# Second attention of a two-layer image tower: the strips of Q and K travel in halves, the heads' scores are dealt out over the body, and the loop over images is written out

## What is computed

```python
q, k, v = jnp.split(src @ in_proj_w.T + in_proj_b, 3, axis=-1)      # 16 heads of 16
scores = jnp.einsum('bhqd,bhkd->bhqk', q, k) / math.sqrt(dh)
ctx = jnp.einsum('bhqk,bhkd->bhqd', jax.nn.softmax(scores, axis=-1), v)
dense_output = ctx.transpose(0, 2, 1, 3).reshape(b, s, d) @ out_proj_w.T + out_proj_b
QK = jnp.einsum('bqr,bkr->bqk', Q, K) / math.sqrt(R)
topv, topi = jax.lax.top_k(jax.nn.softmax(QK, axis=-1), 51)         # a fifth of 257
sparse_attn = zeros_with(topv).normalised()
sparse_output = jnp.einsum('bqk,bkd->bqd', sparse_attn, V)
fused = sig * dense_output + (1.0 - sig) * sparse_output
x = _layernorm(src + fused, ln1_g, ln1_b)
```

## Time and profile before

| | before |
|---|---|
| device time, median of 3 runs | 1273.41 us (1272.54 to 1274.91) |
| the profiled execution | 1266.08 us |
| its span, first to last instruction | 1264.3 us |
| busy over the span | PE 80%, DVE 61%, PEld 59%, POOL 37%, ACT 30% |
| granted TensorE clock, mean | 0.907 of full |
| maximum of a head, L2259 | 128 times 689 ns; idle before it 79.7 us, 79.1 of them until PE's L2503 |
| score matmuls of the heads, L2503 | 256 times 381 ns; idle before them 33.5 us, 19.3 of them until the DMA into fa_ks |
| exponential, L2051 | 128 times 588 ns; idle before it 79.1 us, 77.3 of them until PE's L2568 |

### The profile page before, as it was taken

The page is one execution under the profiler, slowest core; times in us unless marked ns, Lnnn a source line. Parts: engine busy times, 40 slices in busy tenths (PEclk is TensorE's granted clock), DMA queues, the critical chain, the costliest instruction groups (busy, mean ns, idle before and its releaser), DMA issues. The chain is left out here.

```text
span 1264.3 us, 21795 instructions
## 1 busy us (share of the span) xinstructions
PE 1014.5 (80%) x6656; PEld 745.1 (59%) x6656; DVE 765.5 (61%) x1825; ACT 382.2 (30%) x943; POOL 467.4 (37%) x576
## 2 busy tenths in 40 slices
PE   0157989789999965379889789888779997788887
PEld 0155777486776743246556556555369996465555
DVE  7975666554222237367577667556507775688884
ACT  0242433112222221143344344343224442222221
POOL 4972010154000016123233224121136774476664
PEclk9978999759999996689889999898889998899999
DMA  9904500133111112553363463462040000000000
GB/s 316 340 2 142 192 0 1 34 111 116 59 59 60 62 39 64 83 110 105 61 129 94 71 127 91 58 129 92 24 160 1 0 0 1 1 9 17 8 17 18
DMA packets 66590, 94.85 MB, mean 75 GB/s; under 512 B 9176, under 2 KB 58792, under 8 KB 65232
## 3 DMA queue, kind: packets, MB, share of 16 engines
q1 hardware_dynamic: 63312, 85.48, 25.8%
q0 software_dynamic: 3200, 8.43, 2.2%
HBM read 53.28 MB, written 40.34 MB: 74 GB/s over the span
## 5 line engine op out<-in xcount | busy, mean ns | idle before, releaser
L2259 DVE TENSOR_REDUCE fa_nm<-fa_ps 128x2 f32<-128x514 f32 x128 | 82.9, 689 | 79.7 <-PE fa_ps L2503 79.1
L1505 PE MATMUL ex_ps<-we_raw,ex_xT 128*128 x320 | 117.7, 491 | 0.0
L2051 ACT ACTIVATE fa_eT<-fa_ps 128x512 f32<-128x512 f32 x128 | 72.5, 588 | 79.1 <-PE fa_ps L2568 77.3
L2503 PE MATMUL fa_ps<-fa_ks,fa_qs 126*128 126x258 f32 x256 | 65.8, 381 | 33.5 <-DMA fa_ks<-fa_qk_rows 19.3
L3308 PE MATMUL qf_ps<-qf_wg,qf_xT 128*128 128x352 f32 x272 | 90.1, 481 | 2.0 <-ACT qf_xT L3149 1.4
L451 PE MATMUL tk_ps<-tk_u,tk_qb 64*32 64x64 f32 x1024 | 23.9, 268 | 70.5 <-POOLq L318 56.7
L2568 PE MATMUL fa_ps<-fa_qs,fa_ks 128*128 128x256 f32 x256 | 66.0, 351 | 17.5 <-ACT fa_eT L2051 17.5
L1419 DVE COPY ex_hT<-ex_ps 128x384 f32<-128x384 f32 x40 | 22.3, 558 | 92.5 <-PE ex_ps L1514 92.4
L2503 PEld LDWEIGHTS fa_ps<-fa_ks,fa_qs 126*128 126x128 f32 x256 | 46.7, 240 | 49.5 <-issue 29.8
L3308 PEld LDWEIGHTS qf_ps<-qf_wg,qf_xT 128*128 128x128 f32 x272 | 50.7, 195 | 37.4 <-issue 6.8
L2939 PE MATMUL ff_ps<-ff_xT,wg_f 128*128 128x128 f32 x544 | 66.2, 282 | 3.2 <-ACT ff_xT L2838 3.2
(11 more groups left out here) (493 smaller groups left out, 2380.4 us busy)
## 6 DMA issues: line engine op xcount, KB each, us to landing
x_rows<-tk_zero SPq DMA_DIRECT2D x8, 2176.0 KB, 17.5
we_raw<-in_L_ffn_W SPq DMA_DIRECT2D x24, 384.0 KB, 8.1
fa_qs<-fa_qk_rows SPq DMA_DIRECT2D x16, 514.0 KB, 8.2
fa_ks<-fa_qk_rows SPq DMA_DIRECT2D x32, 257.0 KB, 10.4
ex_xin<-x_rows SPq DMA_DIRECT2D x40, 128.0 KB, 2.0
y_rows<-ex_y SPq DMA_DIRECT2D x40, 128.0 KB, 1.7
fa_rsb<-fa_rs_rows SPq DMA_DIRECT2D x32, 132.0 KB, 2.8
fa_qk_rows<-fa_qhl SPq DMA_DIRECT2D x32, 128.5 KB
```

Source lines behind the costliest of these rows:

```text
L1505: last = mm(ps[:, bank + t % 2, 0:HD], xT[:, t % 2, k, :], raw[:, ds(e, 1), m, k * HD:(k + 1) * HD], start=(k == 0), stop=(k == KC - 1))
L2051: cp(eT[:, j % 8, :], ps[:, ST + j % 2, :], ACT.Exp).then_inc(z["e_ready"], 1)
L2259: nc.vector.tensor_reduce(nm[:, :, j], ps[:, b:b + 2, 0:TOK], AX.X, ALU.max, negate=True).then_inc(z["max_done"], 1)
L2503: last = mm(ps[:, b + t, 0:WID], qs[0:TOPS, p, head(j, 1 + t * P, P)], ks[0:TOPS, p, head(j, 0, WID)], start=True, stop=True)
```

## The change

- **Halves.** Everything between projection and strips is done by halves of eight heads: PE, ACT, DVE and POOL in the order Q0, K0, Q1, K1, and in SP's queue eight writes in that order, then the maxima's rows of group 1, then the reads Q0, K0, Q1, K1: two and four DMAs each, of half the columns. Each half has semaphores of its own. Head 0 waits for the first half, head 7 for the second.
- **Heads.** The heads of image u+1 stood in slots 10 to 17, two in each. They now stand in slots 5 to 16, one or two in each; DVE takes the maxima in the slot after. The class query goes from slot 8 to slot 5, ahead of the projection, its maximum on DVE to slot 5, its exponentials on ACT from behind turned score 9 to behind 6. POOL multiplies the class blocks ahead of `shared_context`. The round of slot 5 moves to slot 6. Sparse scores: slot 14; both value products: slots 16 and 17, with DVE's part of both in slot 17.
- **Bodies.** All eight are written out on every engine.

```diff
-    ROUNDS_AT = {0: 1, 1: 1, 3: 1, 4: 1, 5: 1, 7: 1, 8: 1}
+    ROUNDS_AT = {0: 1, 1: 1, 3: 1, 4: 1, 6: 1, 7: 1, 8: 1}
...
-    HEADS_AT = {10: (0, 1), 11: (2, 3), 12: (4, 5), 13: (6, 7), 14: (8, 9), 15: (10, 11), 16: (12, 13), 17: (14, 15)}
-    MAXES_AT = {11: (0, 1), 12: (2, 3), 13: (4, 5), 14: (6, 7), 15: (8, 9), 16: (10, 11), 17: (12, 13, 14, 15)}
+    HEADS_AT = {5: (0, 1), 6: (2,), 7: (3,), 8: (4, 5), 9: (6,), 10: (7,), 11: (8, 9), 12: (10,), 13: (11,), 14: (12,),
+                15: (13, 14), 16: (15,)}
...
     def staged(eng, body):
-        body(0, 0, True, True, True, True)
-        with eng.Fori(0, 2) as i:
-            body(2 * i + 1, 1, False, True, True, True)
-            body(2 * i + 2, 0, False, True, True, True)
-        for u in range(5, BATCH):
-            body(u, u % 2, False, u + 1 < BATCH, u + 2 < BATCH, False)
+        for u in range(BATCH):
+            body(u, u % 2, u == 0, u + 1 < BATCH, u + 2 < BATCH, u + 3 < BATCH)
...
-            def strips_out(u, p, part, a, ready, out, read):
-                sp.wait_ge(z[ready], u + 1)
+            def strips_out(u, p, part, a, c, ready, out, read):
+                sp.wait_ge(z[ready], 2 * u + c + 1)
                 if a == 0 and u >= 2:
                     sp.wait_ge(z[read], 32 * (part + 1) * (u - 1))
                 src, dst = (qhl, khl)[part], d["fa_qk"][part, p, a]
-                for c in range(KC):
-                    sp.dma_start(dst[:, 8 * c:8 * c + 8, :].rearrange("d h n -> h d n"), src[:, a, c, :]).then_inc(z[out], 16)
-
-            def strips_in(u, p, part, out, read):
-                sp.wait_ge(z[out], 64 * (u + 1))
+                sp.dma_start(dst[:, 8 * c:8 * c + 8, :].rearrange("d h n -> h d n"), src[:, a, c, :]).then_inc(z[out], 16)
+
+            def strips_in(u, p, part, c, out, read):
+                sp.wait_ge(z[out], 32 * (u + 1))
                 if u >= 2:
                     sp.wait_ge(z["st_ps"], N * (u - 1))
                 if u:
                     sp.wait_ge(z[read], 32 * (part + 1) * u)
+                cols = slice(8 * c * TOK, 8 * (c + 1) * TOK)
                 src = d["fa_qk"][part, p].rearrange("a d h n -> a d (h n)")
                 if part == 0:
                     for i in range(2):
-                        sp.dma_start(qs[2 * DH * i:2 * DH * (i + 1), p, :].bitcast(F32), src.rearrange("a d n -> (a d) n")
-                                     ).then_inc(z[read], 16)
+                        sp.dma_start(qs[2 * DH * i:2 * DH * (i + 1), p, cols].bitcast(F32),
+                                     src.rearrange("a d n -> (a d) n")[:, cols]).then_inc(z[read], 16)
...
-                    low_parts(u + 1, 1 - p)
+                    low_parts(u + 1, 1 - p, 0)
+                    low_parts(u + 1, 1 - p, 1)
+                    class_blocks(u + 1, 1 - p)
                 if not first:
                     shared_context(u - 1, 1 - p)
                 if more:
-                    class_blocks(u + 1, 1 - p)
                     base(u + 1)
...
-                    queries(u + 1, 1 - p)
-                    keys(u + 1)
+                    for c in range(KC):
+                        queries(u + 1, 1 - p, c)
+                        keys(u + 1, c)
...
                 take_quad(u, p, 0)
                 probs(u, 6)
+                if more:
+                    class_probs(u + 1, 1 - p)
                 probs(u, 7)
                 probs(u, 8)
                 probs(u, 9)
                 take_quad(u, p, 1)
-                if more:
-                    class_probs(u + 1, 1 - p)
                 probs(u, 10)
                 if two:
                     rows(u + 2)
...
-                    if sl == 1 and more:
-                        high_queries(u + 1, 1 - p)
-                    if sl == 2 and more:
-                        high_keys(u + 1)
+                    if more:
+                        for j in HEADS_AT.get(sl - 1, ()):
+                            head_max(u + 1, j)
+                            if j % 8 == 7:
+                                high_maxima(u + 1, j // 8)
+                    if sl in (1, 2) and more:
+                        high_queries(u + 1, 1 - p, sl - 1)
+                        high_keys(u + 1, sl - 1)
                     if sl in (2, 3) and two:
                         mix(u + 2, sl - 2)
+                    if sl == 5 and more:
+                        class_max(u + 1)
+                    elif sl == 5:
+                        class_row_max()
                     if sl in (5, 6) and two:
                         mix(u + 2, sl - 3)
                     if sl == 6 and not first:
                         add_attention(u - 1)
                     if sl == 7 and not first:
                         statistics(u - 1)
-                    if sl == 8 and more:
-                        class_max(u + 1)
-                    elif sl == 8:
-                        class_row_max()
-                    if more:
-                        for j in MAXES_AT.get(sl, ()):
-                            head_max(u + 1, j)
-                            if j % 8 == 7:
-                                high_maxima(u + 1, j // 8)
-                            if j in (13, 15):
-                                values(u + 1, 1 - p, (j - 13) // 2)
-                            if j == 9:
-                                sparse_max(u + 1)
+                    if sl == 15 and more:
+                        sparse_max(u + 1)
+                    if sl == 17 and more:
+                        values(u + 1, 1 - p, 0)
+                        values(u + 1, 1 - p, 1)
...
-                    pe.wait_ge(z["q_in"], 32 * (u + 1))
-                    pe.wait_ge(z["k_in"], 64 * (u + 1))
+                    pe.wait_ge(z["q_in0"], 32 * (u + 1))
+                    pe.wait_ge(z["k_in0"], 64 * (u + 1))
...
+                if j == 7:
+                    pe.wait_ge(z["q_in1"], 32 * (u + 1))
+                    pe.wait_ge(z["k_in1"], 64 * (u + 1))
...
                     if sl == 0 and more:
-                        projected(u + 1, 1 - p, 0, "q_ps")
-                        projected(u + 1, 1 - p, 1, "k_ps")
+                        for c in range(KC):
+                            projected(u + 1, 1 - p, 0, c, "q_ps")
+                            projected(u + 1, 1 - p, 1, c, "k_ps")
...
+                    if sl == 5 and more:
+                        class_query(u + 1)
                     if sl == 5 and not first:
                         project(u - 1, 1 - p)
-                    if sl == 8 and more:
-                        class_query(u + 1)
...
-                            if j == 9:
-                                sparse_scores(u + 1)
-                    if sl in (15, 17) and more:
-                        values(u + 1, 1 - p, (sl - 15) // 2)
+                    if sl == 14 and more:
+                        sparse_scores(u + 1)
+                    if sl in (16, 17) and more:
+                        values(u + 1, 1 - p, sl - 16)
```

More of the change, by code:

```diff
@@ L2136, in _ @@
             act.wait_ge(z["w_ready"], 1)
-            queries(0, 0)
-            keys(0)
+            for c in range(KC):
+                queries(0, 0, c)
+                keys(0, c)
             sparse_operands(0)
@@ L2448, in turn_rows, with projected @@
                 last.then_inc(z["x_ps"], 1)
[L2450 removed]
+            def projected(u, p, j, c, name):
                 pe.wait_ge(z["x_taken"], u + 1)
[L2452 removed]
+                if c == 0 and (not isinstance(u, int) or u):
                     pe.wait_ge(z["max_done"], N * u + j - 1)
[L2454 to L2459 removed]
+                lo = (KC * j + c) * P
+                for k in range(KC):
+                    last = mm(ps[:, SB + 2 * j + c, 0:TOK], w["qk"][:, k, lo:lo + P], xT[:, p, k, :],
+                              start=(k == 0), stop=(k == KC - 1))
+                last.then_inc(z[name], 1)
             def sparse_operands(u, p):
```

109 lines of the change are left out of this document (55 added, 54 removed).

## The result

| | before | after |
|---|---|---|
| device time, median of 4 runs each, side by side | 1274.16 us (1272.54 to 1277.32) | 1333.23 us (1328.59 to 1337.96) |
| ratio | | 1.046, 95% interval 1.042 to 1.050 |
| the profiled execution, its span | 1266.08, 1264.3 us | 1328.59, 1326.9 us |
| granted TensorE clock, mean | 0.907 | 0.900 |
| seven bodies | 331.8 us | 394.8 us |

Slower, as forecast, but by 59 us in place of 28.6, and outside the range of 1279 to 1322. Windows in the columns of the earlier trace rows. After: bodies 0 to 6, then from the stage's first instruction to body 0.

What follows compares the result with a forecast made beforehand. No engine fills a body; a chain through strips and top-8 work, then heads, bounds it. Seven bodies +34.0 and the stretch ahead of body 0 -5.4 give +28.6 on 1273.4: 1302 us, range 1279 to 1322.

Steps and rivals of the forecast that it cites:

- DVE's queue, 12.9 us from head 0 to head 6: Maxima of heads 0 and 1 stand ahead of addition and rounds 4 to 6 on DVE; that stretch takes 12.9 us.
- The idle stretch of 7 us ahead of the first maximum: Sign on DVE: through with slot 5 at t+13.8, it waits some 7 us for head 0, its releaser PE.
- the waits of PE between heads 3 and 6: Sign on PE: it waits for DVE's maxima there, 6 to 8 us a body, with the granted clock low behind it.
- The rival in which DVE is not in the way: Rounds end before strips come, a body takes some 43 us, total 1237 us; chance 0.10.
- Ahead of body 0, -5.4: Before body 0, seven of 16 heads run while the second half lands, saving 5.4 us, between -3 and -6.
- Head 6 to sparse scores, 11.0: PE's remaining heads, turned scores, quads 2 and 3 and small transposes take 11.0 us a body, quad 2 at half clock.
- Writing out, 0 to -1: All eight bodies written out in place of the loop: worth 0 to -1 us.
- First head at t+21.2: In each body PE starts the first head 21.2 us after the body's start, between 19.2 and 22.5.
- the 9.7 us from first read to strips: SP's reads of the first half take 9.7 us, between 9.3 and 10.2, where reading all took 18.7.
- the strips queue up: Rival: twelve reads for six, first half waits behind second half's writes; first head t+24.5, 3.3 us more a body; chance 0.10.
- Sparse scores to next body, 7.5: The end of a body, with both value products now neighbours in slots 16 and 17, takes 7.5 us.
- the forecast's +34.0: Seven bodies, 52.6 us each less 2.4, take 365.8 us against 331.76: 34.0 us more.

Runs made afterwards that it cites:

- the run with the held half: Changed kernel, but SP starts the second half's reads only when the first half's keys have landed; 1319.9 us, ratio 1.036 to the kernel before.
- the second profile of before: The kernel before, unchanged, profiled once more; 1280.4 us, the stage starting at 498.7, seven bodies in 333.1 us.

## Why the prediction was half right

- **DVE's queue, 12.9 us from head 0 to head 6: right.** 12.3 measured, and undoing it gives 52 us back, 35 of them in this stretch. The idle stretch of 7 us ahead of the first maximum is 8.8, the waits of PE between heads 3 and 6 are 5.5 us for 6 to 8 in body 5. The rival in which DVE is not in the way is dead.
- **Ahead of body 0, -5.4: right,** -5.9.
- **Head 6 to sparse scores, 11.0: right,** 10.7. **Writing out, 0 to -1: right.**
- **First head at t+21.2: mis-sized.** 23.3 on average, 24.5 at most and above the bound of 22.5, 14 us in seven bodies. The step that failed is the 9.7 us from first read to strips: I halved the time of the reads as if the other half were not in the same queues. It was 11.3 to 12.2; the run with the held half gives a first head at 21.3. The rival "the strips queue up", to which I gave 0.10 with 3.3 us, comes nearest; the size was 2.1, and it blamed the second half's writes, where the run shows its reads. I had held the equal bytes against it, which says nothing of the order in which they land.
- **Sparse scores to next body, 7.5: mis-sized.** 7.7 in bodies 5 and 6, but 10.1 on average, 18 us in seven bodies. I had taken body 5 of before as the pattern for all, and asked of no row what POOL does beside it. I had put the wait for late increments, which POOL's gathers bring to quad 3 and head 12 in bodies 0 to 4, at nothing. The trace of before shows the gathers beside heads 10 to 12 with no increment late, so it would not have given the price either.
- Together 14.5 + 18.3 - 4.3 - 1.9, and 2.4 that I took off apart for bodies 0 and 6 and that the means hold already, make +29.0 in the bodies: what the forecast's +34.0 lacks of 63.0.
- **The baseline.** I saw that the profiled execution lay 7.3 us under the median and only moved the sum by it. It was the trace of an execution without late increments, and that a new order of POOL and PE might meet them could not be seen from it. Against the second profile of before, held up ahead of the stage as after is, the bodies differ by 61.7 us and the spans by 48.2.
- **The range** was too narrow above: its high end put the first head at 22.5 and left 7.5 for the last part, and the means were 23.3 and 10.1. The 12.5 that it allowed behind head 6, for 10.7 measured, made up for only part of that: 55.4 us a body at the high end, 56.4 measured.
- **The signs.** Bodies were to be 51 to 54 us and are 54.6 to 58.4. DVE's idle stretch, PE's waits for its maxima and the low clock came as named. The wait for the strips was to be nearly gone and is 2.9 to 4.8 us a body in bodies 1 to 6.
- What the forecast never asked was what each half of the change would do alone. Its first term, strips 9 us earlier, is worth 2.1% if the heads stay where they were; 3 of its 9 us are used there (first head at 26.9 for 29.8) before PE's own place for head 0 in its queue decides.

## What to carry to other kernels

When a transfer is made to land earlier, look what stands in each in-order queue ahead of its first consumer: moving the consumer forward puts it in front of work that the old wait had covered, and that work is then on the path. Try the earlier transfer with the old order first; here that gained as much as any kernel tried. Halving a transfer doesn't halve the wait for its first half while the second's reads follow right behind: here 18.7 us for the whole, 12.0 for the first half, and 10.5 with the second held back. And one profile is no baseline for a term that depends on what two engines do at the same moment.
